# Six-layer decoder, first attention: two batches per step, values stationary, sums by a block of ones

## What is computed

```
Q = phi((x @ Wq + bq).reshape(bs, n, H, D)); K = phi((x @ Wk + bk)...); V = (x @ Wv + bv)...
def step(carry, qkv):
    KV = KV + einsum('bhd,bhe->bhde', ki, vi);  Ks = Ks + ki
    num = einsum('bhd,bhde->bhe', qi, KV);      den = einsum('bhd,bhd->bh', qi, Ks)
    return (KV, Ks), num / (den[..., None] + EPS)
return out @ Wo + bo
```

## Time and profile before

| | |
|---|---|
| median of 3 runs | 1488.63 us (1486.94 to 1489.01) |
| the profiled execution | 1494.32 us, of which the span of the profile is 1492.4 us |
| mean granted TensorE clock | 0.951 of full speed |
| TensorE busy | 1389.4 us, 93% of the span |
| VectorE busy | 742.1 us, 50% |
| first attention | from the start to about 365 us |

### The profile page before, as it was taken

One profiled execution on the slowest core, in us unless ns is written; L12 is line 12 of the kernel. 1 busy time (PEld: TensorE's weight loads), 2 busy tenths in 40 slices (PEclk: granted clock), 3 DMA queues, 4 the chain that ended last, 5 costly groups with the idle time before them and its releaser, 6 DMA issues.

```text
span 1492.4 us, 31671 instructions
## 1 busy us (share of the span) xinstructions
PE 1389.4 (93%) x12419; PEld 976.0 (65%) x12419; DVE 742.1 (50%) x1785; ACT 513.7 (34%) x1012; POOL 286.6 (19%) x379
## 2 busy tenths in 40 slices
PE   5899999997899999869996999999998999999984
PEld 4788888885466666536664457575756677777762
DVE  3555555554466666247763212111112555678855
ACT  1112122111255555425663522222121444444432
POOL 1100000000111112078861200000000100224421
PEclk8999999998599999969998999999999999999995
DMA  7500000000022221001210100000000000000001
GB/s 196 89 5 1 0 0 0 0 0 1 15 63 57 55 60 41 2 15 56 77 39 11 53 0 0 0 1 0 0 0 0 3 3 3 15 16 16 16 3 50
DMA packets 35825, 35.83 MB, mean 24 GB/s; under 512 B 11680, under 2 KB 32400, under 8 KB 35712
## 3 DMA queue, kind: packets, MB, share of 16 engines
q1 hardware_dynamic: 35712, 34.23, 9.3%
HBM read 31.61 MB, written 1.86 MB: 22 GB/s over the span
## 4 chain that ended last, share of the span: by engine, by line
PE 87%; ACT 3%; DVE 3%; issue 3%; POOL 2%; DMA 1%; SPq 1%; DVEq 0%; ACTq 0%; POOLq 0%
PE banks L270 46%; PE banks L647 7%; PE banks L633 4%; PE banks L263 4%; PE banks L553 3%; PE banks L787 3%; PE banks L733 3%; PE banks L746 3%; PE banks L782 2%; PE banks L727 2%; PE banks L663 2%; PE banks L525 2%; ACT area L1130 1%; PE banks L772 1%; ACT area L1193 1%
## 5 line engine op out<-in xcount | busy, mean ns | idle before, releaser
L1423 DVE TENSOR_REDUCE Y_room<-banks 112x2 f32<-112x750 f32 x128 | 115.5, 936 | 94.6 <-PE banks L633 94.6
L1500 DVE TENSOR_REDUCE area<-banks 112x8 f32<-112x896 f32 x96 | 100.3, 1086 | 80.9 <-PE banks L733 80.9
L263 PE MATMUL banks<-cst,area 112*128 112x112 f32 x576 | 95.2, 282 | 46.8 <-DVE area L1692 15.5
L270 PE MATMUL banks<-area,room 128*128 128x112 f32 x1024 | 125.2, 286 | 8.5 <-DVE area L1318 6.0
L1130 ACT ACTIVATE area<-banks,Y_room 125x896 f32<-125x896 f32 x96 | 96.7, 1008 | 95.5 <-PE banks L647 95.5
L270 PEld LDWEIGHTS banks<-area,room 128*128 128x128 f32 x1024 | 123.1, 202 | 9.0 <-DVE area L1318 6.2
L1193 ACT ACTIVATE area<-banks 112x896 f32<-112x896 f32 x96 | 82.8, 914 | 121.7 <-PE banks L787 121.7
L263 PEld LDWEIGHTS banks<-cst,area 112*128 112x128 f32 x576 | 65.7, 149 | 85.1 <-issue 61.2
L270 PE MATMUL banks<-room,area 128*112 128x256 f32 (+1 forms) x384 | 119.8, 463 | 0.6 <-ACT area L1083 0.6
L647 PE MATMUL banks<-room,area 64*125 64x224 f32 x768 | 102.8, 388 | 5.2 <-ACT area L1130 3.7
L1626 DVE SCALAR_TENSOR_TENSOR X<-banks,area,X 112x192 f32 (+1 forms) x64 | 26.5, 417 | 160.0 <-PE banks L270 160.0
(11 more groups left out here) (225 smaller groups left out, 2422.9 us busy)
## 6 DMA issues: line engine op xcount, KB each, us to landing
Y_room<-in_ctx SPq DMA_DIRECT2D x16, 375.0 KB
area<-in_ctxT SPq DMA_DIRECT2D x64, 93.8 KB
l<-in_l SPq DMA_DIRECT2D x2, 1024.0 KB, 5.1
room<-in_ctxT SPq DMA_DIRECT2D x16, 112.0 KB, 2.2
out<-X SPq DMA_DIRECT2D x16, 112.0 KB, 1.9
X<-in_x SPq DMA_DIRECT2D x1, 1568.0 KB, 22.8
room<-in_Wq SPq DMA_DIRECT2D x1, 1024.0 KB, 8.4
room<-in_Wk SPq DMA_DIRECT2D x1, 1024.0 KB, 11.3
```

The costliest lines, as they stand in the source:

```text
L263: last = nc.tensor.transpose(dst[:, k * parts:(k + 1) * parts], src[:, k * P:(k + 1) * P], ident[0:parts, 0:parts])
L270: last = nc.tensor.matmul(dst, a, w, start=(k == 0), stop=(k == len(lhs) - 1))
L1423: v_.tensor_reduce(b_nb[u][:, 4 * a + k:4 * a + k + H + 1:H], banks[0:S, 2 * a:2 * a + 2, 0:SC], AX_X, ALU.max, negate=True).then_inc(Bs[" ...
L1500: v_.tensor_reduce(c_nb[:, 8 * i:8 * i + 8].rearrange("q (j n) -> q j n", j=2), banks[0:S, 2 + 2 * i:4 + 2 * i, 0:4 * S].rearrange("q j (n ...
```

## The change

The step is now `phase_a(p)`, for the two batches 2p and 2p+1; it is written out in full instead of in a hardware loop. Per step:

- **Projections.** `project(w, g, m)` has eight groups of two output blocks, each with 224 moving columns (both batches) instead of 112. `a_xn` and `a_xnT` have two buffers each.
- **Sums.** `weighted_a(i)` first multiplies a stationary block of ones (`a_ones`, 113 x 64) with the masked scores `a_at`, 448 moving columns: four products per batch, two per bank, in the column groups 0 and 64. Each sum comes out on all 64 partitions of its head. A row of 1e-6 under `a_at` replaces the addition.
- **Weighted values.** In the same function the values `a_v` of a head (112 x 64) are stationary and the head's masked scores (112 columns) move, in two column groups. The output comes out turned (channels on partitions), so the eight turns of `a_o` and ScalarE's two copies per batch go away.
- **Division.** VectorE's `normalised(b)` takes two reciprocals of 128 x 448 numbers from PSUM and multiplies them into `a_oT` in two instructions of 128 x 448.
- **Banks and waits.** The sums use pb[5] and pb[2], and pb[2] is also a bank of the scores. So `scores(i, x)` waits for both reciprocals of the batch before (`A["rd"]`), and `a_at` may be written again only when its products are done (`A["nd"]`).
- **Beside it.** GpSimd goes through the batches in order, so the normalisation of batch 1 stands behind the addition that waits for `bo`. Two of the four context tiles are filled, and loaded, only after the first attention (`pre["ctx2"]`). The turn of the mask for the cross attention and its copy move into step 2; two casts move from batch 0 to step 1.

```
+                def weighted_a(i):
+                    b = 2 * p + i
+                    pe.wait_ge(A["sm"].sem, A["sm"].at(4 * b + 4))
+                    pe.wait_ge(A["rd"].sem, A["rd"].at(2 * b))
+                    pe.wait_ge(pre["eps"].sem, 2)
+                    heads = a_at.rearrange("k (x j e s) -> k x e j s", x=2, j=4, e=2)
+                    for x in range(2):
+                        for e in range(2):
+                            last = T3.matmul(pb[5 - 3 * x][LD * e:LD * e + LD, 0:4 * S], a_ones, heads[:, x, e], start=True, stop=True,
+                                             tile_position=(0, LD * e))
+                        last.then_inc(A["nd"].sem, 1)
+                    pe.wait_ge(A["nm"].sem, A["nm"].at(2 * b))
+                    pe.wait_ge(A["pj"].sem, A["pj"].at(12 * p + 10 + 2 * i))
+                    for x in range(2):
+                        for j in range(4):
+                            for e in range(2):
+                                h = 8 * x + 2 * j + e
+                                last = T3.matmul(pb[4 + 2 * x][LD * e:LD * e + LD, j * S:(j + 1) * S], a_v[:, h, :],
+                                                 a_at[0:S, h * S:(h + 1) * S], start=True, stop=True,
+                                                 tile_position=(0, LD * e))
+                        last.then_inc(A["nd"].sem, 1)
...
+                def scores(i, x):
+                    b = 2 * p + i
+                    pe.wait_ge(A["ph"].sem, A["ph"].at(8 * p + 4 * (x + 1)))
+                    pe.wait_ge(A["sm"].sem, A["sm"].at(4 * b + 2 * x))
+                    pe.wait_ge(A["rd"].sem, A["rd"].at(2 * b))
...
+                def normalised(b):
+                    for x in range(2):
+                        dve.wait_ge(A["nd"].sem, A["nd"].at(4 * b + x + 1))
+                        v_.reciprocal(a_rd[:, x * 4 * S:(x + 1) * 4 * S], pb[5 - 3 * x][:, 0:4 * S]).then_inc(A["rd"].sem, 1)
+                    for x in range(2):
+                        dve.wait_ge(A["nd"].sem, A["nd"].at(4 * b + x + 3))
+                        dve.wait_ge(A["rd"].sem, A["rd"].at(2 * b + x + 1))
+                        dve.wait_ge(A["wd"].sem, A["wd"].at(b))
+                        v_.tensor_tensor(a_oT[:, x * 4 * S:(x + 1) * 4 * S], pb[4 + 2 * x][:, 0:4 * S],
+                                         a_rd[:, x * 4 * S:(x + 1) * 4 * S], ALU.mult).then_inc(A["nm"].sem, 1)
...
+            def phase_a(b):
+                ln_rstd(A, b, 2)
+                pool.wait_ge(A["xn"].sem, A["xn"].at(b + 1))
+                pool.wait_ge(ld["bo"].sem, 16)
+                g_.tensor_tensor(xb_(b), xb_(b), bo0, ALU.add).then_inc(A["xb"].sem, 1)
```

More of the change, by code:

```diff
@@ L412, in _ @@
             sp.wait_ge(pre["bx"].sem, 1)
-            for n in range(4):
+            for n in range(2):
+                context(n, n)
+            sp.wait_ge(pre["ctx2"].sem, 1)
+            for n in range(2, 4):
                 context(n, n)
@@ L487, in _ @@
             T3 = nc.tensor
[L490 to L504, removed]
-                if on(b - 1):
-                    pe.wait_ge(A["nm"].sem, A["nm"].at(3 * b))
-                    for g in range(2):
-                        transposes(a_o[:, g * 512:(g + 1) * 512], S, 4, pb[2 + g]).then_inc(A["ot"].sem, 1)
-                if on(b):
-                    for g in range(2):
-                        pe.wait_ge(A["pj"].sem, A["pj"].at(6 * b + 3 + g))
-                        if isinstance(b, int) and b == 0:
@@ new lines, in phase_a @@
+                if p == 0:
+                    normed(0)
+                if p < B // 2:
+                    pe.wait_ge(A["xte"].sem, A["xte"].at(p + 1))
+                    for g, (w, m) in enumerate(((wq0, 0), (wq0, 2), (wk0, 0), (wk0, 2), (wq0, 4), (wq0, 6), (wk0, 4), (wk0, 6))):
+                        project(w, g, m)
+                    scores(0, 0)
+                    values(0)
+                    scores(0, 1)
+                if p > 0:
+                    output(2 * p - 1)
+                if p == 2:
+                    pe.wait_ge(A["xu"].sem, A["xu"].at(2 * p))
+                    pe.wait_ge(pre["rowbias"].sem, 1)
+                    for c in range(NKC):
+                        last = T3.transpose(pb[7][0:KC, c * B:(c + 1) * B], mask_f[:, c * KC:(c + 1) * KC], ident[0:B, 0:B])
+                    last.then_inc(Bs["kt"].sem, 1)
@@ L558, in _ @@
+                if p < B // 2:
+                    weighted_a(0)
+                    scores(1, 0)
+                    values(1)
+                    scores(1, 1)
+                    if p == 2:
+                        pe.wait_ge(Bs["ke"].sem, 1)
+                    output(2 * p)
+                    if p + 1 < B // 2:
+                        normed(p + 1)
+                    weighted_a(1)
             pe.wait_ge(ld["cst"].sem, 16)
-            batches(pe, phase_a, 1)
+            for p in range(B // 2 + 1):
+                phase_a(p)
@@ L1383, in _ @@
-            batches(dve, phase_a, 1)
+                normalised(2 * p + 1)
+                if not more:
+                    residual_a(B - 1)
+            for b in range(2):
+                stats_of(A, b, 1, 0)
+                normed(b)
+            dve.wait_ge(ld["bias"].sem, 32)
+            v_.tensor_scalar(bqk0[:, :], bqk0[:, :], 1.0, None, ALU.add).then_inc(pre["bias1"].sem, 1)
+            dve.wait_ge(pre["bias1"].sem, 1)
+            dve.wait_ge(ld["cst"].sem, 16)
+            for p in range(B // 2):
+                phase_a(p)
```

291 lines of the change are left out of this document (141 added, 150 removed).

## The result

| | before | after |
|---|---|---|
| median of 4 runs | 1488.33 us (1486.94 to 1489.01) | 1532.91 us (1530.44 to 1540.05) |
| ratio, 95% interval | | 1.030 (1.027 to 1.033) |
| profiled execution; its span | 1494.3; 1492.4 us | 1530.4; 1528.5 us |
| first projections start | 10.20 us (batch 0 alone) | 33.74 us (batches 0 and 1) |
| last residual addition of the first attention ends | 364.75 us | 408.30 us |

The changed kernel is 3% slower. 1548 us was forecast, with 1505 to 1605 as the range. The traced execution of the kernel before is 6.0 us longer than its median and that of the kernel after 2.5 us shorter than its own, so whole times are compared by medians, and the lengths of parts (the last three rows) are those of one execution each.

What follows compares the result with a forecast made beforehand. TensorE bounded the kernel; waiting for long reciprocals, a step would take 38.1 + 5.7 of stalls + 3.3 of clock = 47.1 us. Eight steps and the start gave +59: 1488.6 + 59 = 1548 us, range 1505 to 1605.

Steps and rivals of the forecast that it cites:

- VectorE becomes the place that sets the step: First attention: TensorE, 93% busy before, would wait for new work on VectorE, which had 11.03 us per 20 us.
- R: Time of one 128x448 reciprocal on VectorE, taken as 2.81 us, with 0.70 and 5.5 us as ends.
- rival 3: Reciprocal surplus of 78 ns is paid once, 0.70 us each; both stalls vanish, step 38.1 us, 1470 us; chance 0.17.
- rival 2: Reciprocals of 3.9 us (1582 us) or two clock falls per step (1574 us), both together 1609 us; chance 0.20.
- The stalls: TensorE waits per step: 3.5 us at scores after both reciprocals, 2.2 us at the next step's first bias addition.
- TensorE's own step: TensorE's work for two batches without waits: 38.1 us, 2.7 us less than 40.84 before.
- rival 4: Column groups with 64 columns of weights don't run side by side: step 43.7 us, 1520 to 1534 us; chance 0.03.
- The clock: Stalls lower TensorE's granted clock: one fall per step, costing 3.3 us, between 0 and 6.6.
- rival 1: The clock holds through both stalls: step 43.8 us, 1522 us; chance 0.13.
- The start: First projections wait for batch 1's normalisation, behind the addition waiting for `bo`, and start at 36.6 us.
- The tail: Last weighted sums to last residual addition: 4.7 us waiting and 6.6 us output product, the same as 10.9 before.
- The rest of the program: Unrolled code, exponentials, later context tiles and moved mask turn lie beside TensorE's work: costed at nothing, uncovered 0 to 3 us.

Runs made afterwards that it cites:

- e1: Changed kernel with a plain copy in place of each 128x448 reciprocal, division left out: 1467.2 us, 0.985 of the kernel before.
- e5: Changed kernel with the second batch's values ahead of its first scores and the output product ahead of its second scores, VectorE's order following: 1496.4 us.
- e4: Changed kernel with GpSimd computing batch 1's normalisation factor before the addition that waits for `bo`: 1512.9 us, 1.015 of the kernel before.
- e11: e7 with the mask's turning back at the start of the cross attention, as in the kernel before: 1466.4 us.
- e7: Changed kernel with the three reorderings of e4, e5 and e6 together: 1467.5 us, 0.985 of the kernel before.
- e3: Changed kernel with eight unread products added on TensorE in the first stall, before the second batch's scores: 1520.1 us, 1.021 of the kernel before.
- e9: Changed kernel with ScalarE's exp(-ln x) for VectorE's reciprocal, the edits of e4 and e5, and each bank's sums waiting for its own masks only: 1452.4 us.
- e2: Changed kernel with the reciprocal taken of 224 of each 448 numbers and the other 224 copied: 1478.2 us, 0.993 of the kernel before.
- e6: Changed kernel with the next step's first two bias additions ahead of VectorE's two multiplications at a step's end: 1520.2 us, 1.020 of the kernel before.

## Why the prediction was right, point by point

**VectorE becomes the place that sets the step: shown.** Predicted from the full TensorE and the half-full VectorE of before, shown by e1, in which one short instruction stands in the place of each reciprocal and every wait, bank and product stays.

**R, the reciprocal: 2.81 predicted, 2.93 measured, 4% off.** The reading of a surplus that grows with the count held, per number 6.14 ns against the assumed 5.9. Both far ends (0.70 and 5.5) are out, and with them rival 3; so is the 3.9 of rival 2. The Trainium skill's repeat count of 8 ("VectorE: DVE Perf Modes", "First, the fixed hardware budget"), taken as eight cycles a number, gave an estimated 3.7 us; the row shows 2.93. By the page's 0.96 GHz, 6.14 ns is an estimated 5.9 cycles.

**The stalls: right.** 3.5 predicted and 3.68 measured eight times; 2.2 predicted and 1.90 measured, six of seven times (once 1.96). The sum for the eight steps had the second stall eight times, though it lies between two steps: one too many, 2.2 us. The queueing was as described: behind the waiting scores stood all of the second batch, and e5, which only moved what did not have to wait, took the first stall away.

**TensorE's own step: 38.1 predicted, 37.5 in e1.** 224 columns take 12.37 us for 64 records, 0.193 each, as interpolated (12.35). Sums 1.56 and weighted values 1.64 us, together 3.2 where 3.3 were predicted; rival 4 (no column groups side by side) is out. Two thirds of the 0.6 us were extra prices for changes of grouping, which I had put too high.

**The clock: the mechanism right, the size too high.** One fall per step was put at 3.3 us, between 0 and 6.6. After the first stall the clock fell each time (rival 1, that it holds, is out), and it came back sooner than the 6 to 7 us assumed: the scores and values behind it lost 1.6 to 1.7 us in six steps (1.22 and 5.16 us instead of 1.04 and 3.69 in the one shown), 3.1 in the first and 2.9 in the third. After the second stall it held in five of seven steps, and in the other two, with a stall of much the same length, the 48 records took this:

```profile
264.93 11.03 PE L269 MATMUL banks<-area,room 128*128 128x224 f32 x48 [1.90 <-DVE area L1350]
```

instead of 9.35 us. So the eight steps lost 15.9 us behind first stalls and 3.4 behind second ones, 2.4 us per step instead of 3.3, and the first projections at the low clock lost 1.7 (14.05 us instead of 12.37) where 3.3 was put: 20.9 us instead of 29.7. This is the term of the sum that was mis-sized most, by 8.8 us. It was sized with the falls at 42.83 us and at 355.99 us in the kernel before, where less dense work stood around them; why the clock came back sooner here isn't shown. From the start of the projections to the last weighted sums the kernel took 364.2 us against 376.5 forecast, 12.3 less: 8.8 are the clock, 2.9 the two stalls (2.2 of them the one counted too often), and only 0.6 all the rest. What TensorE's own step had too much (4.8 us) was mostly taken back by things put at nothing: 1.24 us of waiting for a mask in the first step, 1.0 us for the mask's turning in step 2, and some 0.3 us per step around the stalls, of which the cause isn't shown.

**The start: 36.6 predicted, 33.74 measured.** The bias arrived 3.4 us earlier (GpSimd's addition at 28.74 instead of 32.11); the order was as described, and e4, whose projections start at 12.05 us, shows that it was this wait. The loads at the start landed at differing times: in the traces of the six kernels that keep this order the projections started between 33.7 and 38.1 us.

**The tail: 10.9 predicted, 10.4 measured.** 4.59 us of waiting (4.7 predicted) and an output product of 5.31 us:

```profile
402.53 5.31 PE L269 MATMUL banks<-room,area 128*112 128x256 f32 x16 [4.59 <-DVE area L1377]
```

**The rest of the program: costed at 0 to 3 us, 7.4 us shorter between the two traces, near 1 us longer by the medians.** The traces differ in the clock at the head of the cross attention. Stretches of 15 us from the last residual addition on, before and then after (length, busy us of each engine, PEclk):

```profile
364.75:379.75 15.00, 9.54 (x37) 4.47 (x39) 7.32 (x15) 2.56 (x5) 1.49 (x4) 0.57 0.00 0
379.75:394.75 15.00, 12.67 (x53) 5.84 (x49) 7.92 (x14) 2.31 (x4) 2.33 (x4) 0.50 0.10 27
394.75:409.75 15.00, 13.67 (x108) 7.36 (x105) 5.18 (x11) 5.28 (x6) 2.33 (x4) 0.56 0.01 3
```

```profile
408.30:423.30 15.00, 9.73 (x40) 4.07 (x40) 8.39 (x18) 2.32 (x4) 4.93 (x7) 0.64 0.40 56
423.30:438.30 15.00, 12.27 (x51) 6.37 (x53) 7.51 (x13) 3.32 (x5) 2.07 (x5) 0.50 0.08 27
438.30:453.30 15.00, 14.22 (x179) 8.35 (x175) 7.79 (x11) 7.31 (x9) 0.93 (x1) 0.83 0.20 38
```

In the third stretch TensorE runs at 0.83 instead of 0.56 and gets 179 records done instead of 108. In the trace of the kernel before the low clock lasts 41 us there, in that of the kernel after 31. Summed over the first 60 us of the rest, (1 - granted clock) times the length is 20.5 us before and 15.3 after: 5.2 of the 7.4.

That is a difference between two executions, and it isn't shown to be one between the kernels. The traced execution of the kernel before took 1494.3 us at a mean granted clock of 0.951. Of its 27 executions that were timed beside the experiments, 23 took 1486.5 to 1490.5 us at 0.953 to 0.955, and only four took 1491.4 to 1493.5 at 0.951 or 0.952. So the trace shows one of the rare long ones, about 5 us of clock worse than usual, which is the size of the difference in question. The low clock there lasts 37.5 us in e1, 34 in e11 and 30 to 34 in the others, so it varies among the changed kernels too. Taken from the medians (less the first attention of the trace and the 1.9 us between time and span), the rest is an estimated 1121.7 us before and 1122.7 after, within the 0 to 3 us of the prediction. This estimate takes the first attention to be as long in the other executions as in the traced one. A second trace of the kernel before would settle it, and there is none. The expectations of e1, e7 and e11, which took the 7 us for an effect of the change, rest on the same pair of traces.

**The sum.** The first attention was forecast 15.7 us too long: 12.3 of steps, 2.9 of start and 0.5 of tail. The medians give the same: +59 forecast, +44.6 measured, 14.8 us between them. So nothing is left over for the rest of the program. The range held the result, the mechanism is the forecast's, and the number alone would not have told it from rival 1: 1532.9 lies 15 us from the forecast and 11 from rival 1's 1522. What tells them apart are the stretched records behind each first stall, and e3.

## What to carry to other kernels

Moving a small per-row division to the large, turned side multiplies it: 16 numbers cost 0.25 us on VectorE and 448 cost 2.93, at 6.1 ns each, almost five times an addition of the same shape (0.62 us). Before turning an output, count the numbers that have to be divided, and if they stay many, let ScalarE take exp(-ln x) for them. When an engine must wait for such a result, first move ahead of the wait what does not need it: moving the values ahead of the scores alone brought 36 us back, and some of that was the clock that a stall takes along.

## What the runs showed of the hardware

- The price of a reciprocal on VectorE, 6.14 ns per number and 0.17 us (1.550 us for 128x224, 2.926 us for 128x448).
- Logarithm and exponential over 128x448 on ScalarE take 0.541 and 0.568 us, and a batch had one table load of 1.283 us in front of its two logarithms and one in front of its two exponentials; the first operation started within 0.01 us of the load's end.
- The granted clock after a wait of TensorE in the first attention, by the time of the records behind it: lower after each of the eight waits of 3.7 us and after the waits of 4.6, 2.7 (e9) and 2.4 us (e2) at the end; lower after two of the seven of 1.9 to 2.0 us (three of seven in e3 and two in e4 and e5 each, for waits of the same length); at the full level after the eight of 1.41 us (e2) and the seven of 0.84 us (e6, e7). The scores and values behind a stall of 3.68 us lost 1.6 to 1.7 us in six of eight steps.
- Eight products in place of an equally long wait made the kernel 12.8 us faster without doing anything else.
